# A selective-scan and mixture-of-experts layer: the pieces of each step in another order, dt clipped by halves, u and z behind fewer waits

## The reference, cut to what matters

```python
x = x + mamba(layernorm(x))     # x: 32 sequences of 256 tokens, 128 wide
x = x + moe(layernorm(x))
# mamba: xz = x @ in_proj.T; xc, z = split(xz)          (256 channels each)
#   u  = causal_conv(xc, 4 taps, 256 -> 256 channels) + b
#   dt = clip(sigmoid(u @ dt_w.T + dt_b), 1e-4, 1.0)
#   B, C = u @ B_w.T, u @ C_w.T                         (16 states)
#   state = exp(clip(dt * A, -5, 5)) * state + dt * B * u + 1e-6   (per channel, state, token)
#   y = sum_n(state * C) + D * u;  out = (y * silu(z)) @ out_w.T
# moe: shared expert + top 2 of 8 routed experts: (silu(x @ wg) * (x @ wu)) @ wd
```

## Time and profile before

| | us |
|---|---|
| median of 3 runs | 1402.33 (1399.95 to 1402.63) |
| the profiled execution, its time | 1403.58 |
| its span, first to last instruction | 1401.9 |
| around the span | 1.68 |
| PE busy | 1217.3 (87% of the span) |
| DVE busy | 1177.6 (84%) |
| ACT busy | 901.7 (64%) |
| POOL busy | 847.7 (60%) |

### The profile page before, as it was taken

The page is one execution under the profiler, slowest core; times in us unless marked ns, Lnnn a source line. Parts: engine busy times, 40 slices in busy tenths (PEclk is TensorE's granted clock), DMA queues, the critical chain, the costliest instruction groups (busy, mean ns, idle before and its releaser), DMA issues.

```text
span 1401.9 us, 27101 instructions
## 1 busy us (share of the span) xinstructions
PE 1217.3 (87%) x8709; PEld 1022.8 (73%) x8709; DVE 1177.6 (84%) x2236; ACT 901.7 (64%) x1452; POOL 847.7 (60%) x1354
## 2 busy tenths in 40 slices
PE   6779897899989898998989898998989999787883
...
GB/s 178 1 1 9 1 9 9 20 117 73 109 82 127 35 143 108 41 124 99 121 63 118 62 143 87 56 130 89 130 61 68 112 95 98 95 174 178 244 274 89
DMA packets 111646, 132.29 MB, mean 94 GB/s; under 512 B 10128, under 2 KB 82704, under 8 KB 111504
## 3 DMA queue, kind: packets, MB, share of 16 engines
...
q0 software_dynamic: 8192, 16.79, 4.2%
...
## 4 chain that ended last, share of the span: by engine, by line
PE 42%; DVE 26%; ACT 13%; issue 11%; DMA 3%; POOL 3%; SPq 1%; DVEq 0%; POOLq 0%; ACTq 0%
DVE h L1279 11%; DVE yT L1297 10%; PE p_hT L1053 7%; PE p_db L1036 7%; PE p_misc L1060 6%; PE p_dn L1216 4%; PE p_gu L1204 4%; ACT dA L872 3%; PE p_gu L1195 3%; ACT L969 2%; ACT hm L969 2%; PE p_misc L1097 2%; POOL ysel L791 2%; ACT dBT L929 2%; PE p_misc L1113 1%
## 5 line engine op out<-in xcount | busy, mean ns | idle before, releaser
L1279 DVE TENSOR_TENSOR_SCAN h<-dA,p_db 128x512 f32<-128x512 f32 x512 | 603.7, 1204 | 66.1 <-PE p_db L1036 64.7
L735 POOL TENSOR_SCALAR dBT<-wT,bcT 128x256 f32<-128x256 f32 x704 | 340.1, 483 | 347.8 <-ACT wT L903 138.0
L1297 DVE SCALAR_TENSOR_TENSOR yT<-p_hT,bcT,yT 128x256 f32<-128x256 f32 x960 | 402.9, 471 | 40.4 <-PE p_hT L1053 40.4
L872 ACT ACTIVATE dA<-dt_sb,A_sb 128x510 f32<-128x510 f32 x512 | 333.0, 711 | 27.7 <-DVE h L1279 26.4
L1036 PE MATMUL p_db<-ident,dBT 128*128 128x128 f32 x2048 | 300.8, 278 | 57.0 <-DVE h L1279 53.3
L1036 PEld LDWEIGHTS p_db<-ident,dBT 128*128 128x128 f32 x2048 | 238.5, 143 | 112.9 <-issue 102.9
L1053 PE MATMUL p_hT<-ident,h 128*128 128x128 f32 x2048 | 290.2, 281 | 25.3 <-DVE yT L1297 14.0
L1053 PEld LDWEIGHTS p_hT<-ident,h 128*128 128x128 f32 x2048 | 237.9, 145 | 64.6 <-issue 31.5
L929 ACT ACTIVATE dBT<-wT,eps,bcT 128x256 f32<-128x256 f32 x320 | 163.9, 592 | 0.0
L777 POOL DMA_INDIRECT xs_dram<-xn,slot x128 | 127.4, 995 | 54.7 <-issue 35.9
L791 POOL DMA_INDIRECT ysel<-ys_dram,slot x128 | 123.8, 968 | 56.5 <-issue 32.4
...
## 6 DMA issues: line engine op xcount, KB each, us to landing
...
xs_dram<-xn,slot POOLq DMA_INDIRECT x128, 2.3
```

What stands on the lines that cost most here:

```text
L735: op = pool.tensor_scalar(dBT[:, j % DBT_RING, c], wT[:, g % 2, c], bcT[:, g % 2, c, n:n + 1], STATE_EPS, ALU.mult, ALU.add)
L872: act.activation(dst[:, :, 1:], src[:, :, 1:], ACT.Exp, scale=A_sb[:, half, n:n + 1]).then_inc(exp_done, 1)
L1279: dve.tensor_tensor_scan(h[:, j % 2, half], dA[:, j % DA_RING, half], p_db[half][:], 0.0, ALU.mult, ALU.add).then_inc(scan_done, 1)
L1297: op = dve.scalar_tensor_tensor(yT[:, g % 2, cc], p_hT[pair][:, c], bcT[:, g % 2, cc, NS + n:NS + n + 1], yT[:, g % 2, cc], ALU.mult, ALU.add)
```

## The change

The tables of all five engines are rewritten. On PE the `U`, `G`, `N`, `xnT`, `v0` and `op` that stood behind or between `i0` and `i1` now stand ahead of both, in 10 of the 16 slots; one `U` goes from slot 3 to behind `h` in slot 4; `h` of slot 5 goes behind `i1`. On ACT several `x` come a slot earlier, `E` comes ahead of `V`, `sig` comes behind two `x`, and in slot 9 `E` stands ahead of `bc`. On POOL `c`, `d` and `gate0` come earlier and `clip` becomes `clip0` and `clip1`, one for each half. On DVE a `P` goes ahead of `y0` (slot 4), a `y1` between `s0` and `s1` (slot 9), a `P` ahead of an `r` (slot 13), a `Q` (adding the shared expert) ahead of `y0` (slot 15). On SP `T` stands ahead of the `W`s in slot 14 (was behind them), `Y` ahead of `W` in slots 5 and 11, and other `W`s later. Slots are counted from 0. The plan, the order in which `p_misc` is used and all instructions but the clip are the same. In the first step `z0` and `z1` go behind the first `i0` and `i1`; `u0` no longer waits for the mixer weights, `dt0` does; and `dt0` needs only `u0` emptied, its second half only `u1`.

```diff
--- before.py
+++ after.py
@@ -66,34 +66,34 @@
 
 
 PE_SLOTS = (
-    "U h N i0 G i1 X", "h U yb0 i0 N i1 yb1 G", "X h U i0 xnT i1 N G", "h u0 N U i0 v0 i1 X X U",
-    "N h G i0 op i1 X", "U G h u1 v1 i0 G N h i1", "U X xn2T i0 G i1 dt0 f0 X",
-    "N h dt1 f1 N U i0 i1 logit X G", "h N U i0 i1 G bc N X", "h i0 U i1", "h G G N X U z0 i0 i1 z1",
-    "h X N U G i0 i1 X U rank", "N h i0 i1", "h G X wT0 U N wT1 G i0 i1 h X N X", "i0 U N i1 G h G",
-    "i0 U i1 X")
+    "U h N G i0 i1 X", "h U yb0 N i0 i1 yb1 G", "X h U xnT i0 i1 N G", "h u0 N U v0 i0 i1 X X",
+    "N h U G op i0 i1", "U X G h u1 v1 G N i0 i1 h", "U X xn2T G i0 i1 dt0 f0 X",
+    "N h dt1 f1 N U i0 i1 logit X G", "h N U i0 i1 G bc N X", "h U i0 i1", "h G G N X U z0 i0 i1 z1",
+    "h X N U G i0 i1 X U rank", "N h i0 i1", "h G X wT0 U N wT1 G i0 i1 h X N X", "U G N i0 i1 h G",
+    "U i0 i1 X")
 DVE_SLOTS = (
     "stats1 s0 s1 y0 P y1", "C Q s0 s1 Q P yd0 y0", "s0 s1 yd1 y1 Q C y0 y1", "s0 C C y0 s1 P y1 P Q",
-    "s0 s1 y0 P y1 x1 C", "stats2 s0 s1 C y0 Q Q P y1", "s0 s1 y0 P y1", "s0 y0 s1 C Q y1 s0 lg P Q",
-    "s1 Q C y0 P C", "s0 s1 y1 r y0 r y1 r P r r s0 r", "Q C s1 r y0 y1 r P r Q r s0 s1 r",
-    "r y0 r P y1 r C C Q r", "s0 r s1 r y0 y1 r r", "C r P r s0 s1 Q r y0 y1 r Q r",
-    "r r C s0 P s1 r r y0 r P y1", "s0 C s1 C y0 Q Q P y1")
+    "s0 s1 P y0 y1 x1 C", "stats2 s0 s1 C y0 Q Q P y1", "s0 s1 y0 P y1", "s0 y0 s1 C Q y1 s0 lg P Q",
+    "s1 Q C y0 P C", "s0 y1 s1 r y0 r y1 r P r r s0 r", "Q C s1 r y0 y1 r P r Q r s0 s1 r",
+    "r y0 r P y1 r C C Q r", "s0 r s1 r y0 y1 r r", "C P r r s0 s1 Q r y0 y1 r Q r",
+    "r r C s0 P s1 r r y0 r P y1", "s0 C s1 C Q y0 Q P y1")
 ACT_SLOTS = (
-    "x x d V x m0 d X", "E m1 V d", "x X xnT d V", "E x E X V d", "u0 X x E X E u1 V d", "x d V x E X",
-    "xn2T V X", "dt0 E d d dt1 sig x V X", "E x X d V", "E x d bc E V", "x V z0 z1 d E X",
-    "x X X E V d d V d", "x wT0", "E x wT1 V X X", "x E V X d", "X E V E")
+    "x x d x V m0 d E X", "m1 V x d", "X xnT d E V", "x E X V d", "u0 X x E E X u1 V x d", "V x E d X",
+    "xn2T V X", "E dt0 d dt1 x d V E x sig X", "X d E V", "d E bc x x V", "V z0 z1 E d x X",
+    "X E X V d d d x V", "E x wT0", "wT1 V X X", "x E V X d", "E X E V")
 POOL_SLOTS = (
-    "", "d d c c S d c c C C ln1", "", "d C c d gate0 gate1 c C S S", "d C S S", "C c ln2 c C d d d C S", "",
-    "c c c c S d clip S C S d C d C S", "", "", "c c w0 w1 C S d S", "C", "", "c d S C c d S", "",
-    "d C C S S")
+    "c", "c d d S d c c ln1 gate0 C C", "", "c d C c d gate1 C S S", "d C S c c S",
+    "C C ln2 d d d c c C c c S", "", "clip0 S d clip1 S C S d C d c c C S", "", "", "w0 w1 C S d c S", "C",
+    "", "d c S C d d S", "", "C C S S")
 SP_SLOTS = (
-    "", "W W W Y T", "T Y O W", "Y xl Y W T", "O O T O T Y", "W W T Y Y", "", "W Y T T T O O O", "",
-    "O W W T Y Y W W", "", "Y O T O W O T O W Y", "", "Y Y W", "W T T O O O", "Y Y O T T")
+    "", "Y T W W xl Y W", "T", "Y O Y W T", "O W T O O", "T Y T Y W W", "", "Y Y T W T T", "",
+    "T O O O O Y W W", "", "Y Y W O W T T O O W", "", "Y Y W O", "Y T T W W", "T O O Y Y O O T")
 
 PE_FIRST = (
-    "xnT u0 v0", "u1 v1 dt0 f0", "dt1 f1 bc", "wT0 wT1 z0 z1", "h i0 i1 N G U X", "h i0 i1 N G U X",
+    "xnT u0 v0", "u1 v1 dt0 f0", "dt1 f1 bc", "wT0 wT1", "h i0 i1 N G U X", "h i0 i1 N G U X",
     "h i0 i1 N G U X", "h i0 i1 N G U X", "h i0 i1 N G U X", "h i0 i1 N G U X", "h i0 i1 N G U X",
     "h i0 i1 N G U X", "h i0 i1 N G U X", "h i0 i1 N G U X", "h i0 i1 N G U X", "h i0 i1 N G U X",
-    "h i0 i1 N G U X", "h i0 i1 N G U X", "h i0 i1 N G U X", "h i0 i1 N G U X")
+    "h i0 i1 N G U X", "h i0 i1 N G U X", "h i0 i1 N G U X", "h i0 i1 N G U X z0 z1")
 DVE_FIRST = (
     "s0 s1 y0 y1 P Q C",) * 16
 ACT_FIRST = (
@@ -102,8 +102,8 @@
     "V X E", "V X E", "V X E", "V X E", "V X E", "V X E", "V X E", "V X E", "V X E", "V X E", "V X E",
     "V X E")
 POOL_FIRST = (
-  "clip w0 w1", "c d S", "c d S", "c d S", "c d S", "c d S", "c d S", "c d S", "c d S", "c d S", "c d S",
-  "c d S", "c d S", "c d S", "c d S", "c d S", "c d S")
+    "clip0 w0 clip1 w1", "c d S", "c d S", "c d S", "c d S", "c d S", "c d S", "c d S", "c d S", "c d S",
+    "c d S", "c d S", "c d S", "c d S", "c d S", "c d S", "c d S")
 SP_FIRST = (
   "xl", "T W Y O", "T W Y O", "T W Y O", "T W Y O", "T W Y O", "T W Y O", "T W Y O",
   "T W Y O", "T W Y O", "T W Y O", "T W Y O", "T W Y O", "T W Y O", "T W Y O",
@@ -745,15 +745,15 @@
                 pool.tensor_tensor(yT[:, g % 2, chunks], yT[:, g % 2, chunks], y_more[:, chunks], ALU.add
                                    ).then_inc(more_added, 1)
 
-            def clip_dt(g):
-                pool.wait_ge(misc_emptied, max(misc_at["dt0", g], misc_at["dt1", g]))
-                pool.tensor_scalar(dt_sb[:, g % 2], dt_sb[:, g % 2], 1.0, DT_MIN, ALU.min, ALU.max
+            def clip_dt(g, half):
+                pool.wait_ge(misc_emptied, misc_at[f"dt{half}", g])
+                pool.tensor_scalar(dt_sb[:, g % 2, half], dt_sb[:, g % 2, half], 1.0, DT_MIN, ALU.min, ALU.max
                                    ).then_inc(dt_ready, 1)
 
             def weigh_u(g, half):
 
+                pool.wait_ge(dt_ready, HALVES * g + half + 1)
                 if half == 0:
-                    pool.wait_ge(dt_ready, g + 1)
                     at_least(pool, misc_in_psum, misc_at["wT1", g - 1] if g else 0)
                 pool.tensor_tensor(w_sb[:, half], dt_sb[:, g % 2, half], u_sb[:, g % 3, half],
                                    ALU.mult).then_inc(w_ready, 1)
@@ -824,8 +824,8 @@
                             pool.wait_ge(xs_stored[b % 2], 32 * sum(SHARED[c] for c in range(b % 2, b + 1, 2)))
                         layer_norm(behind, xn2[:, behind % 4], x1[:, behind % X1_RING], mv2, rs2, nm2,
                                    ln2_mv, ln2_step, xn2_ready)
-                    if name == "clip" and ahead is not None:
-                        clip_dt(ahead)
+                    if name in ("clip0", "clip1") and ahead is not None:
+                        clip_dt(ahead, int(name[4]))
                     if name in ("w0", "w1") and ahead is not None:
                         weigh_u(ahead, int(name[1]))
                     if name in ("m0", "m1") and u - NS * k < BY_ACT - 1:
@@ -862,7 +862,7 @@
 
                 g, n = divmod(j, NS)
                 if n == 0:
-                    act.wait_ge(dt_ready, g + 1)
+                    act.wait_ge(dt_ready, HALVES * (g + 1))
                 if j == 0:
                     act.wait_ge(starts_zeroed, 1)
                 at_least(act, scan_done, 2 * (j - DA_RING) + 2)
@@ -1067,6 +1067,7 @@
                 if name in ("u0", "u1"):
                     convolve(g, half, 1).then_inc(misc_in_psum, 1)
                 else:
+                    pe.wait_ge(misc_emptied, misc_at["u1", g])
                     pe.matmul(misc_bank(name, g), wdt_sb[:, 1, half * P:(half + 1) * P], u_sb[:, g % 3, 1],
                               start=False, stop=True).then_inc(misc_in_psum, 1)
 
@@ -1081,7 +1082,6 @@
                         mm = pe.transpose(bank[:, c * P:(c + 1) * P],
                                           yT[:, g % 2, c, half * P:(half + 1) * P], ident[:])
                 if name == "u0" and g == 0:
-                    pe.wait_ge(mixer_weights, 16 * len(mixer_loads))
                     pe.wait_ge(amin_ready, 1)
                     pe.wait_ge(misc_emptied, misc_at["xnT", 0])
                     pe.matmul(p_dn[0:1, 0], amin[:], ident[:], start=True, stop=True).then_inc(amin_in_psum, 1)
@@ -1109,7 +1109,9 @@
                         mm = pe.transpose(bank[:, c * P:(c + 1) * P], xn2[:, g % 4, c], ident[:])
                 if name in ("dt0", "dt1"):
                     half = int(name[2])
-                    pe.wait_ge(misc_emptied, misc_at["u1", g])
+                    if g == half == 0:
+                        pe.wait_ge(mixer_weights, 16 * len(mixer_loads))
+                    pe.wait_ge(misc_emptied, misc_at["u0", g])
                     pe.matmul(bank, wdt_sb[:, 0, half * P:(half + 1) * P], u_sb[:, g % 3, 0], start=True, stop=False)
                     return
                 if name == "logit":
```

## The result

The changed kernel takes 1398.59 us (median of 8, 1396.16 to 1400.52) where the kernel before takes 1401.70 (median of 8); the ratio is 0.9974, 95% interval 0.9963 to 0.9985. So it is faster by 0.26%, about 3.1 us, a little under half of the 6.8 forecast.

The account below looks back on a forecast made before the run. PE bounds the first half of a step with routed quads, DVE the second. Terms -1.9 + 1.3 - 0.7 - 5.5 = -6.8 on the profiled 1403.58 give 1396.8, as median 1395.5 us; range 1390 to 1402.5.

Parts of the forecast that it names:

- The start: Up to the first scan: earlier u0 and clip by halves give 2.5 us, less 0.6 for z0 and z1; -1.9.
- I let 0.6 of the gain go there: Start: z0 and z1 behind the first inputs, emptied by ACT with its silu load, cost 0.6 us.
- Steps 0 to 3: v0 and op ahead of both inputs delay scans, y1 between scans gives some back; +1.3 us, bounds 0 and +2.9.
- Steps 4 to 14: Costs of 0.5 us, a gain of 1.2 from P waits, other moved pieces at 0; -0.7, bounds -2 and +1.
- The -1.2 for the `P` wait: Slot 15: U ahead of i0 removes DVE's 0.31 us wait of a P, four such waits; -1.2 us.
- Step 15: T issued first and pieces moved on PE and ACT fill waits; -5.5 us, between -2.2 and -6.5.
- The doubt about `W` behind `Y`: SP in step 15: four W behind a Y store come some 6 us later, just as G wants them.
- the shift passes through unchanged: Behind step 15: its critical T load keeps its place relative to its step, so step 15's shift carries through.
- The sign of being wrong: Even and odd step together over 0.5 longer than 160.9; G waiting for wring in step 15; DVE waiting on L1204.
- A: Step 15's gain mostly does not arrive (W behind Y hold G up, or tail loads lag); 1399.5 us, chance 0.21.
- B: Slots 3 and 4: v0 and op delay the scan by 0.75 in all 15 steps; +3.1, 1405.5 us, chance 0.10.
- C: Even steps: the two added ACT table loads are not hidden; +18.2 less 6.8, 1413.7 us, chance 0.03.

Follow-up runs that it names:

- run 6: Tables of the kernel before in all 16 steps, with changed start waits, clip by halves, z0 and z1 ahead of the inputs; 1398.24 us, ratio 0.9971.
- run 12: Kernel of run 5 with dt clipped in one instruction, as before the change; 1437.19 us on a slower chip, ratio 0.9882 to the kernel before.
- Run 10: Kernel of run 5 with v0 and op back between i0 and i1; 1438.93 us on a slower chip, ratio 0.9897 to the kernel before.
- run 5: Changed kernel with both repairs: z0 and z1 ahead of the first i0, wT0 ahead of x in ACT's slot 12; 1391.40 us, ratio 0.992.
- run 8: Kernel of run 5 with the tables of before in steps 0, 1 and odd steps 3 to 13; 1390.91 us, ratio 0.9913 to the kernel before.
- run 9: Kernel of run 5 with sig ahead of the two x in ACT's slot 7 again; 1445.72 us on a slower chip, ratio 0.9952.

## Why the prediction was right or wrong, point by point

**The direction and the seat of the gain: right.** Faster was given 0.66, and step 15 carries it. Size: twice too large. Two places lost what the sum had at 0.6 and at nothing, the `z` pieces (3.3 us) and `wT0` behind two `x` (4.7 in steps 4 to 14), and gains that the sum did not have made up for most of it: 2.4 us behind step 15, and what run 6 shows with the tables of before as well, 3.1 in step 15, 1.1 in steps 1 to 3 and 2.4 in steps 4 to 14 (of which 1.2 was in the sum, as the `P` waits). That the time ended inside the range owes something to luck.

**The start: right up to its last step.** The first matmul of `u0` can't start before `xnT` is emptied, and that emptying began between 11.3 and 13.3 us from one run to another, so I count from there. To the start of step 1 it took 91.44 us before (12.29 to 103.73) and 88.89 in run 6 (12.75 to 101.64), which has the changed start with the `z` pieces in their old place: 2.55 less, where 2.5 was forecast. Only 1.3 of it is there at the first scan; the rest comes in the first units. The clip gave less than said: POOL's products end 2.5 us behind dt's second half instead of 3.7, 1.2 less where I had 1.8, and run 12 says that 0.2 to 0.7 of it arrives. The step that failed is "I let 0.6 of the gain go there" for `z0` and `z1`. I followed them on ACT, where they are emptied, and not on PE, where they had filled a wait for POOL and now stand, at the low clock with 1.9 us each, ahead of the inputs of unit 1. It measured 3.3.

**Steps 0 to 3: v0 and op sized right, wT0 missing.** Run 10 gives 0.84, 0.37, 0.35 and 0.04 for `v0` and `op` where I had 0.7 and three times 0.4. `y1` between the scans gives 0.4 in step 0, as said (run 5 against run 6, unit 9 to unit 10), and 0.1 or less in each of steps 1 to 3. That steps 1 to 3 came to -0.3 instead of +1.0 is a sum of things that I did not have: 1.1 less that run 6 shows with the tables of before as well, 0.9 more for `wT0`, and 0.9 given back by the rest of the tables, which no run takes apart.

**Steps 4 to 14: wrong, a missing term.** I listed `v0`, `op`, `U`, `sig` and the POOL and SP pieces, and costed ACT's earlier `x` at nothing by not costing it at all. What is moved ahead of a piece delays it: I applied that to PE and to `sig`, but not to `wT0`, which now had two `x` ahead of it. It is worth 0.87 in each odd step, 4.4 of the 5.5 they lost. `xnT` ahead of `i0`, 0.1 in my sum, is the likely seat of the rest: PE waits 0.46 for its bank, works without a pause up to slot 7 and is 0.43 late there, and the step is 0.44 longer in run 5 (76.33) than with the table of before (75.89); no run moves `xnT` alone. The -1.2 for the `P` wait was right in size: step 8 takes 84.39 with the old table and the half clock, 83.83 with the old table and the full clock, 83.76 in run 8 with the new table and the half clock, and 0.2 of these are the routing instruction's. But its cause lay a level lower, in a stretch at a granted clock of 0.5, which the row of a wait alone doesn't show; without that stretch the new tables give an even step 0.1. Of the zeros, `sig` measured a gain and the clip's second instruction nothing. With `wT0` mended, steps 4 to 14 take 883.8 us by the new tables (run 5) and 883.6 by the old ones (run 6).

**Step 15: right in seat, partly by luck in size.** Up to the scan of unit 14 it became 7.2 us shorter, and 6.0 up to the last scan, against 5.5. But run 6 has 3.1 of the 7.2 with the old tables; between runs 6 and 5 it is 4.0, 2.4 by SP's order, where I had 2.2 for the X's wait, and 1.6 by the other engines', where I had 3.3. What failed is that second part: the order on PE and ACT was sized from waits, of which the first fell from 2.17 to 1.00 by itself in run 6. The doubt about `W` behind `Y` did not come true: they were issued 5.3 later, and PE never waited. And "the shift passes through unchanged" did not hold: the last `T` came 7.7 earlier relative to the step's first scan, 1.7 more than the last scan did, and the X's wait of 2.5 for it is gone; what follows the last scan takes 2.4 less. How much of that is chance is open: it takes 110.6 to 113.5 in six kernels with the same tables from step 15 on, and the 193.7 to 196.3 of the others from step 15 to the end says 2 us or so may be, which is also most of what lies between the 4.7 of the profiles and the 3.1 of the medians.

**The sign of being wrong.** An even and an odd step together were to stay within 0.5 of 160.9, which was the length of steps 8 and 9; they take 161.24. Steps 4 and 5, 6 and 7, 10 and 11 had 160.1 to 160.3 before and are 0.7 to 0.8 longer. So the sign was there in them, and it stood for neither A nor B but for `wT0`.

**Rivals.** A's sum (1399.5) lay 0.9 from the result, nearer than the forecast's 3.1, but for another reason: not step 15 gave back its gain, but step 0 and the odd steps took half of it. B and C were refuted by runs 10 and 9. The Trainium skill, page "ScalarE: Activation LUTs", section "Rules for kernel authors", has functions grouped by table; run 9 does that, with 14 loads of 1.28 us fewer, and is the slowest of its four: this case does not bear the rule out where the grouped function waits for its input (2.10 us in step 4).

**A better version.** Both repairs keep the rest of the change and measure 0.992 of the kernel before, 1391.4 us; so two pieces' places were worth more than the whole change had gained (0.4 to 0.5% against 0.3 to 0.4%).
